# Two attention stages of one kernel: maxima ahead of the full-array matmul, output copies between the exponentials, another fetch order on SyncE

## What is computed

```python
x = x + _L0_conv_ref(_gn(x), ...)     # window attention: 4 variants (2 shifts x 2 strip directions), 8 heads of 8
x = x + _L1_conv_ref(_gn(x), ...)     # gated depthwise 3x3 convolution
t = _to_tokens(x)
t = t + _L2_attn_ref(_ln_t(t), ...)   # attention over 1024 tokens, 16 heads of 8
t = t + _L2_ffn_ref(_ln_t(t), ...)    # 8 experts, gelu, top 2
t = t + _L3_attn_ref(_ln_t(t), ...)   # local attention
t = t + _L3_ffn_ref(_ln_t(t), ...)    # 8 experts, silu, top 2
# both attentions of this case:
attn = softmax(q @ k.T); out = attn @ v
```

## Time and profile before

| | us |
|---|---|
| median of 3 runs (4228.9 to 4235.95) | 4231.09 |
| the profiled execution | 4227.69 |
| its span, first to last instruction | 4225.8 |
| `window_attention`, 128 steps | 336 to 820 |
| `token_attention`, 512 steps after a lead-in | 1172 to 2692 |
| TensorE's mean granted clock | 0.925 |

### The profile page before, as it was taken

One profiled execution on the slowest core, in us unless ns is written; L12 is line 12 of the kernel. 1 busy time (PEld: TensorE's weight loads), 2 busy tenths in 40 slices (PEclk: granted clock), 3 DMA queues, 4 the chain that ended last, 5 costly groups with the idle time before them and its releaser, 6 DMA issues. The chain is left out here.

```text
span 4225.8 us, 66475 instructions
## 1 busy us (share of the span) xinstructions
PE 3397.3 (80%) x24463; PEld 1531.3 (36%) x24463; DVE 2491.0 (59%) x4085; ACT 1933.4 (46%) x2321; POOL 841.4 (20%) x861
## 2 busy tenths in 40 slices
PE   6988777557687777777777777769988649999999
PEld 4655554324211111111111111343476524444444
DVE  3227766365688888888888888334377323333333
ACT  1215666512156666666666666524333223233332
POOL 0001333400000000000000000014400035555555
PEclk9997889778799999999999999869988779999999
DMA  4444544300400000000000000014300022232221
GB/s 138 135 119 94 114 110 109 76 1 23 157 11 15 23 21 15 20 15 25 14 20 14 20 25 5 8 63 150 120 1 0 28 91 80 86 97 83 86 82 47
DMA packets 137544, 247.17 MB, mean 58 GB/s; under 512 B 34808, under 2 KB 47264, under 8 KB 136800
## 3 DMA queue, kind: packets, MB, share of 16 engines
q1 hardware_dynamic: 137312, 243.98, 20.2%
HBM read 171.55 MB, written 56.62 MB: 54 GB/s over the span
## 5 line engine op out<-in xcount | busy, mean ns | idle before, releaser
L1073 DVE TENSOR_REDUCE mxv<-mx_ps 128x1 f32<-128x512 f32 x2048 | 1279.7, 682 | 238.2 <-PE mx_ps L932 238.1
L1048 ACT ACTIVATE PT<-st_ps 128x1024 f32<-128x1024 f32 x1024 | 992.4, 1021 | 447.9 <-PE st_ps L945 442.0
L932 PE MATMUL mx_ps<-KS,QS 24*128 24x512 f16 x2048 | 538.1, 391 | 317.9 <-DVE mxv L1073 300.6
L1916 DVE TENSOR_TENSOR u<-h_ps,s 128x512 f32<-128x512 f32 x352 | 243.4, 691 | 541.5 <-ACT s L1891 495.3
L959 PE MATMUL o_ps<-PT,VA 128*32 128x512 f32 x4096 | 546.4, 605 | 1.1 <-ACT PT L1048 0.9
L1953 POOL TENSOR_TENSOR hg<-u,gb 128x512 f32<-128x512 f32 x352 | 451.6, 1285 | 378.9 <-DVE u L1916 296.6
L1891 ACT ACTIVATE s<-h_ps 128x512 f32<-128x512 f32 x352 | 210.2, 597 | 595.7 <-PE h_ps L1865 595.7
L667 DVE TENSOR_REDUCE mxv<-mx_ps 128x4 f32<-128x512 f32 x512 | 319.8, 683 | 146.4 <-PE mx_ps L542 140.0
L1873 PE MATMUL y_ps<-hg,w 128*128 128x512 f32 x704 | 361.5, 597 | 55.2 <-POOL hg L1953 55.2
L932 PEld LDWEIGHTS mx_ps<-KS,QS 24*128 24x128 f16 x2048 | 137.3, 91 | 568.2 <-DVE mxv L1073 530.8
L945 PE MATMUL st_ps<-QS,KS 26*128 26x512 f16 x2048 | 327.0, 382 | 1.0 <-ACT PT L1048 0.2
(11 more groups left out here) (231 smaller groups left out, 4155.8 us busy)
## 6 DMA issues: line engine op xcount, KB each, us to landing
gb<-g SPq DMA_DIRECT2D x64, 512.0 KB, 3.7
gb<-g SPq DMA_DIRECT2D x16, 2048.0 KB
QK<-qk SPq DMA_DIRECT2D x128, 192.0 KB
qk<-hl SPq DMA_DIRECT2D x80, 256.0 KB, 3.3
RB<-d SPq DMA_DIRECT2D x48, 256.0 KB, 3.5
qk<-hl SPq DMA_DIRECT2D x64, 128.0 KB, 3.3
v<-vs SPq DMA_DIRECT2D x32, 256.0 KB, 3.2
VS<-v SPq DMA_DIRECT2D x32, 256.0 KB, 3.3
```

The source lines that it names most:

```text
L932: nc.tensor.matmul(mx_ps[:, use % 3, :], rows(QS, g // 2, j, STACK)[:, t * C:(t + 1) * C], rows(KS, g // 2, j, STACK)[:, half * HALF:(half ...
L1048: nc.scalar.activation(PT[:, n % 2, 2 * a:2 * a + 2], st_ps[:, a], ACT.Exp, scale=1.0 / SHIFT ** 2).then_inc(st_free[a], 1)
L1073: nc.vector.tensor_reduce(mxv[:, g % 2, j, t, half:half + 1], mx_ps[:, slot], AX.X, ALU.max).then_inc(mx_free, 1)
```

## The change

It moves instructions, and adds and removes none. In both stages A and B are issued at the head of a step, in front of the wait for `st_free[0]` and of the full-array matmul; C and D stay behind the second pair of scores. The output copy goes between the two exponentials: in `window_attention` the copy of step n-2 stands there in step n (before: the copy of n-1 behind both exponentials of step n), and in `token_attention` the copy of a finished group stands there in the second step of the next group (before: at the end of its first step). SyncE's order in `window_attention` is now stacks, rows, denominators; the stacks wait for the last scores of the group that used them. VectorE's reciprocal in `token_attention` moves from step 4 to step 6.

```diff
 # window_attention, SyncE
                     for u in range(U):
-                        if u:
-                            load_den(i, u - 1)
-                        elif kind != "first":
-                            load_den(i - 1, 3)
+                        sp.wait_ge(st_ready[1], i * STEPS + 4 * u)
                         if u == 0 and kind != "first":
                             load_qk(i, 3)
...
                         if u:
+                            load_den(i, u - 1)
                             regroup(i, u - 1)
                         elif kind != "first":
+                            load_den(i - 1, 3)
                             regroup(i - 1, 3)
 # both stages, TensorE
                         for a, pair in enumerate(PAIRS):
+                            if a == 0:
+                                for j in pair:
+                                    ahead(j)
                             pe.wait_ge(st_free[a], i * STEPS + (n + 1))
...
                             scores(n, a)
-                            for j in pair:
-                                ahead(j)
                             if a:
+                                for j in pair:
+                                    ahead(j)
                                 continue
 # window_attention, ScalarE
-                        if n:
-                            take(i, n - 1)
-                        elif kind != "first":
-                            take(i - 1, STEPS - 1)
+                            if a == 0 and n > 1:
+                                take(i, n - 2)
+                            elif a == 0 and kind != "first":
+                                take(i - 1, STEPS + n - 2)
 
                 periods(act, image)
+                take(LAST, STEPS - 2)
                 take(LAST, STEPS - 1)
 # token_attention, ScalarE
-                        if n % KT == 0:
-                            if n:
-                                take(i, n // KT - 1)
-                            elif kind != "first":
-                                take(i - 1, G - 1)
+                            if n % KT == 1 and a == 0:
+                                if n > KT:
+                                    take(i, n // KT - 1)
+                                elif kind != "first":
+                                    take(i - 1, G - 1)
 # token_attention, VectorE
-                        if n == 4 and kind != "first":
+                        if n == 6 and kind != "first":
```

## The result

The changed kernel takes **4372.7 us** (median of 4 runs, 4364.62 to 4392.33) against 4232.1 us before (4 runs): a ratio of 1.034 [1.031, 1.038], slower by 3.4%. The forecast was 4337 with a range of 4130 to 4430. The profiled execution took 4369.63 us, its span 4367.8, at a mean granted clock of 0.854 (before 0.925).

The account below looks back on a forecast made before the run. It saw waits for reductions ahead of D bounding the window step, and a closed circle through the reductions the token step. 4227.7 + 131 (window) - 25 (token) = 4334, plus 3.4 for the median: 4337 us, range 4130 to 4430.

Parts of the forecast that it names:

- Part 1: Token stage: A and B first shorten the step from 2.85 to 2.52 us, saving 164 us.
- my circle: Token stage's plain step with A and B first: 0.46 + 0.75 + 0.31 + 1.00 = 2.52 us.
- Part 2: Token stage: values wait for the moved copy in each group's second step, 1.25 us later, 63 times: 79 us lost.
- Part 3: Window stage, both moves: the copy sets a step of 3.81 us, 0.83 more; 485 us for the stage at full clock.
- The term taken on trust: Window step: A and B to the full-array matmul, 0.32 us from the row of D, floor 0, ceiling 0.64.
- the estimate without a drain: Window step: A and B's term would be 0.22 us without any TensorE drain, the stage 12 us shorter.
- Part 4: Window stage, SyncE's order and longer groups: 40.7 us of waits for rows go; up to 41 us return if not.
- Part 5, the clock in the window stage: Window stage: the pause lowers the clock for three quarters of the time, steps of 5.31 us there, +131 us.
- Part 5, the clock in the token stage: Token stage: 200 us at the low level cost some 60 us, bounds 0 and 150; stage -25 us.
- Rival 1: The clock holds in both stages: 4146 us, from 4105 to 4185; chance 0.20.
- Rival 4: The copy does not hold the values; window step falls towards 2.52 us, the whole to about 4000; chance 0.03.
- Rivals 2 and 3: Clock low in part of window stage only, 4185 to 4275, chance 0.11; whole window and half token stage, 4450 to 4550, 0.06.

## Why the prediction was right, point by point

The sign, the mechanism and the range held; the time is 36 us above the forecast. It would have been more, were it not for a compensation: the window stage and the token stage's clock cost 23 and 37 us more than I had, and the token stage's maxima gained 20 us more. That the sum came so near owes something to luck.

- **Part 1, the token stage's maxima.** Expected -164 us for steps of 2.52; measured -184.5 with the maxima alone, at 2.48 us. One term of my circle was 0.04 too long: the reduction starts 0.42 us after A, not 0.46. TensorE's and VectorE's rows in the kernel after show it, with VectorE idle until A is there: A, reduction, D (its weight load), values, A again.

```profile
2001.62 0.39 PE L935 MATMUL mx_ps<-KS,QS 24*128 24x512 f16 x2
...
2002.04 7.45 DVE L1079 TENSOR_REDUCE mxv<-mx_ps 128x1 f32<-128x512 f32 x12 [0.48 <-PE mx_ps L935]
...
2002.79 0.09 PEld L935 LDWEIGHTS mx_ps<-KS,QS 24*128 24x128 f16 x1 [0.42 <-DVE mxv L1079]
2003.11 1.06 PE L962 MATMUL o_ps<-PT,VA 128*32 128x512 f32 x8
...
2004.11 0.39 PE L935 MATMUL mx_ps<-KS,QS 24*128 24x512 f16 x2
```

- **Part 2, the token stage's copy.** Expected +79 us; +77.2 with the pause filled. The step that waits for the copy is 3.68 to 3.73 us where I had 3.77.
- **Part 3, the window circle.** Expected 3.81 us, measured 3.81. The term taken on trust, 0.32 for A and B ahead of the full-array matmul, measured 0.34 (432.68 to 433.02). The whole stage at the full clock was to be 485 us; with the pause filled it is 493.0. Of the drain in the Trainium skill ("TensorEngine Tiling (Array Packing)", Tiling Modes, Key Properties) the row bears out the sign only: 0.34 is more than the 0.22 of the estimate without a drain. No run here separates the drain from the rest of the 0.34.
- **Part 4, SyncE.** The 40.7 us went, as expected, but by the longer groups and not by the new order: with the old order they went too. I had named both causes and not weighed them.
- **Part 5, the clock in the window stage.** A step at the low clock was put at 5.31, and is 5.31. The share of the time at the low level was put at three quarters; it is 513.0 of 629.1 us, four fifths. That is the first mis-sized term: +153.8 us instead of +131. Some 5 of these 23 us are no matter of the clock: I had subtracted a window of 484 us, which is wider than the 128 steps in it. The pause itself was put at about 1.2 us and is 1.23 at the full clock and 1.32 at the low one. The last image's steps, put at 4.8 us, took 4.76.
- **Part 5, the clock in the token stage.** I took 200 us at the low level and some 60 us, a third of them less a little, as the price. It was 285.4 us, and the price 97.2, a third indeed: the share held and the time at the low level was mis-sized. This is the larger of the two misses. With the larger gain of part 1 the stage came out at -10 instead of -25.
- **The pages on the clock.** The profile shows a clock that went between its two levels in a loop with a short pause in each step, and filling the pause held it at 0.99. The Trainium skill ("TensorE: Matmul & The Clock Gate", A second HAM failure mode: psum-queue depth-cycling) tells of such swings; by that page the time was the forecast's, and the trace agrees, with 513.0 of the window stage's 629.1 us at the low level, in spells between spells at the full one.
- **The rivals.** Rival 1, the clock holds, was put at 4146 us. It did not happen, but the filled kernel makes that case true by force, and took 4137. Rival 4, that the copy would not hold the values, is refuted by 127 waits in 128 steps. Rivals 2 and 3 lie below and above what the clock did.

What I had not seen is how little it takes: the moved copy alone, with A and B beside the scores, has the low clock for 257.5 us (before 139.8), though its step is 0.3 us shorter and its holes are two smaller ones:

```profile
402.80 0.39 PE L542 MATMUL mx_ps<-QK 24*128 24x128 f16 x4 [0.57 <-DVE mxv L668]
...
403.70 1.08 PE L571 MATMUL o_ps<-PT,VA 128*32 128x128 f32 x32 [0.50 <-ACT OR L636]
```

This is TensorE's timeline in the copy-only kernel: 0.57 us ahead of D and 0.50 ahead of the values. The forecast counted only on the long pause. Nor can I say what makes one 3.8 us step keep the full level and the next lose it; in the changed kernel stretches of 3.4 to 13.7 us at the full clock lie between stretches of 17 to 37 us at the low one.

## What to carry to other kernels

An engine that is ahead of its work is not a free place: moving ScalarE's copy in front of the second exponential put it on the path of TensorE, lengthened the plain window step from some 2.6 us (with the maxima in front) to 3.81, and opened a pause; filling that pause gave back 233 us of the two stages. Count the pause that an edit opens on TensorE, not only the step; where a pause can't be avoided, matmuls into a bank that is free anyway can be a cheap test of how much of a loss is the clock. They are no sure cure: with the copy alone they halved the time at the low clock and gave nothing. A bundle of three moves deserves a run of each alone: here one was worth 191 us and hidden beneath another's loss, and two waits in one chain (SyncE's store, GpSimd's order) paid in full only when both were taken away. And a stage that turns faster can run into the next wait: with the maxima in front the plain window step fell by 0.4 us, and longer waits for rows and more time at the low clock took most of the gain.

## What the runs showed of the hardware that I had not expected

- Additional work on TensorE made the kernel shorter by some 230 us: eight matmuls per window step, 0.62 us together, raised the granted clock of the stage from 0.59 to 0.99, and the same in one token step of eight raised it there from 0.91 to 1.00.
- The pause does not shrink when TensorE becomes slower: 1.32 us at the low clock, 1.23 at the full one. ScalarE sets it, whose exponential and copy take 1.02 and 0.46 to 0.48 us at either clock.
- VectorE's reductions, a mean of 682 ns each in the page, start 0.60 us apart when nothing holds them: six take 3.67 us in the row below, from the token stage of the kernel after, so their records overlap by 0.08 us. Four of them have a floor of 2.39 us and not of four times 682 ns. The plain steps of 2.48 us stay above it; they follow TensorE's circle.

```profile
1354.03 3.67 DVE L1079 TENSOR_REDUCE mxv<-mx_ps 128x1 f32<-128x512 f32 x6
```
